# Value product from three fp16 products of high and low parts, with the low part made on VectorE

## What is computed

```python
A  = einsum('mi,bhis->bhms', Wa, xh) + ba
Bm = einsum('ni,bhis->bhns', Wb, xh) + bb
V  = einsum('ni,bhis->bhns', Wv, xh) + bv
attn_maps = softmax(Bm, axis=-1)       # over the pixels
attn_vecs = softmax(V, axis=2)         # over the 64 channels of a head
G = einsum('bhms,bhns->bhmn', A, attn_maps)
Z = einsum('bhmn,bhns->bhms', G, attn_vecs)
x = x + Z                              # then group norm, filters, add
```

## Time and profile before

| | us |
|---|---|
| median of 3 runs | 14357.67 (14353.88 to 14361.22) |
| profiled execution | 14358.22 |
| its span, first to last instruction | 14356.5 |
| TensorE busy | 13503.8 (94%) |
| ScalarE busy | 11121.4 (77%) |
| GpSimd busy | 9729.7 (68%) |
| VectorE busy | 9540.1 (66%) |

### The profile page before, as it was taken

How to read it: one execution, slowest core, us unless ns; L and a number is a source line. 1 busy time by engine, 2 the same in 40 slices (tenths; PEclk the granted TensorE clock), 3 DMA queues, 4 the chain that set the end, 5 groups by cost and what they waited for, 6 DMA issues and landing times.

```text
span 14356.5 us, 399601 instructions
## 1 busy us (share of the span) xinstructions
PE 13503.8 (94%) x158336; PEld 11965.0 (83%) x158688; DVE 9540.1 (66%) x23485; ACT 11121.4 (77%) x20736; POOL 9729.7 (68%) x16823
## 2 busy tenths in 40 slices
PE   7999999999999999999999999999999999999999
PEld 6888888888888888888888888888888888888888
DVE  6666666666666666666666666666666666666665
ACT  6777777777777777777777877777777777777777
POOL 5666666666666676666766667666676666766667
PEclk9999999999999999999999999999999999999999
DMA  3234222343223432234322343223432234322242
GB/s 90 77 101 108 77 74 76 99 108 81 75 75 95 108 84 75 75 92 108 90 73 75 87 108 93 74 75 86 105 97 75 74 83 105 102 73 75 78 105 58
DMA packets 1998658, 1242.80 MB, mean 87 GB/s; under 512 B 79748, under 2 KB 1931140, under 8 KB 1996804
## 3 DMA queue, kind: packets, MB, share of 16 engines
q1 hardware_dynamic: 1996804, 1217.21, 32.6%
HBM read 570.85 MB, written 268.44 MB: 58 GB/s over the span
## 4 chain that ended last, share of the span: by engine, by line
PE 65%; DVE 18%; ACT 11%; issue 6%; SPq 0%; DMA 0%; POOL 0%; DVEq 0%; POOLq 0%
PE ps L1145 64%; DVE nblk L870 4%; ACT t L664 4%; DVE t L1046 3%; ACT yb L696 3%; DVE z L1052 2%; DVE nrun L874 2%; DVE srun L858 2%; ACT z L679 2%; DVE mrun L859 2%; ACT xn L669 1%; DVE pt L864 1%; DVE bexp L877 1%; ACT yr L702 1%; PE ps L1197 0%
## 5 line engine op out<-in xcount | busy, mean ns | idle before, releaser
L1145 PE MATMUL ps<-dn_t,yb 128*128 128x64 f32 (+1 forms) x32768 | 5057.5, 255 | 0.0
L1145 PEld LDWEIGHTS ps<-dn_t,yb 128*128 128x128 f32 x32768 | 4701.4, 191 | 18.4 <-issue 14.8
L494 POOL TENSOR_SCALAR yb<-yb 128x532 f32<-128x532 f32 x4096 | 2587.1, 632 | 1761.9 <-ACT yb L696 1740.9
L1046 DVE TENSOR_TENSOR t<-ps,t 128x266 f16<-128x266 f32 x4096 | 1752.5, 432 | 2698.9 <-ACT t L664 2595.8
L1145 PE MATMUL ps<-up,xn 128*128 128x266 f16 x12288 | 3275.1, 278 | 50.8 <-DVE t L1046 11.2
L664 ACT ACTIVATE t<-ps 128x266 f16<-128x266 f32 x4096 | 1589.1, 393 | 2099.9 <-PE ps L1145 2044.0
L696 ACT ACTIVATE yb<-ps,bias_b 128x532 f32<-128x532 f32 x4096 | 2860.4, 699 | 56.9 <-PE ps L1145 51.9
L1145 PE MATMUL ps<-up_a,t 128*128 128x138 f16 x15360 | 2030.1, 223 | 310.4 <-DVE t L1046 309.5
L1052 DVE TENSOR_TENSOR z<-ps,z 128x512 f16<-128x512 f32 x2048 | 1416.5, 692 | 943.1 <-ACT z L679 898.3
L1145 PE MATMUL ps<-up_b,p 128*128 128x138 f16 x15360 | 2023.3, 223 | 0.0
L1145 PEld LDWEIGHTS ps<-up,xn 128*128 128x128 f16 x12288 | 1724.8, 141 | 228.6 <-DVE t L1046 125.5
(11 more groups left out here) (168 smaller groups left out, 27876.5 us busy)
## 6 DMA issues: line engine op xcount, KB each, us to landing
xc<-in_x SPq DMA_DIRECT2D x512, 512.0 KB, 4.7
xh<-in_x SPq DMA_DIRECT2D x480, 512.0 KB, 5.7
p<-t SPq DMA_DIRECT2D x1920, 128.0 KB, 2.5
out<-xh SPq DMA_DIRECT2D x480, 512.0 KB, 3.2
t<-t SPq DMA_DIRECT2D x960, 128.0 KB, 2.5
xn<-in_x SPq DMA_DIRECT2D x64, 512.0 KB, 5.1
xh<-in_x SPq DMA_DIRECT2D x64, 256.0 KB, 3.0
out<-xh SPq DMA_DIRECT2D x64, 256.0 KB, 2.6
```

Of the source, the lines that this page charges most:

```text
L494: nc.gpsimd.tensor_scalar(v, v, CLAMP, -CLAMP, ALU.min, ALU.max).then_inc(s_yc, 1)
L1046: nc.vector.tensor_tensor(t1[:, par, 1, i, :], ps[:, bank, 0:UP], t1[:, par, 0, i, :], ALU.subtract).then_inc(s_t1, 1)
L1145: return nc.tensor.matmul(o, l, r, start=start, stop=stop, skip_group_check=share)
```

## The change

The block is now normalised fully when it is gathered: `centre` has `scale=r0, bias=nmr0`, so the weights need no scaling, and `wvs`, `wvh` and their two instructions a unit go. The weights are split once, at the program's start, into `wv_2`: high part in fp16, low part the fp16 of the rest. `cast` writes the block's high part in fp16 into `xcs[r][:, 0]`. A new step of VectorE, `value_low`, writes the low part, `xcb[r]` minus the high part, into `xcs[r][:, 1]`, and a new semaphore `s_xw` tells of it. `value` waits for that and makes high x high, low weights x high, high weights x low, each in fp16 with 512 columns. `v_t` takes the high parts. The buffers lie in a half of `t1` that the stage doesn't use.

```diff
...
             def attention(u):
...
                 def centre(k, r):
                     act.activation(xcb[r].rearrange("p (w h) -> p w h", w=WB), xc_wh[:, bass.ts(k, WB), :], ACT.Identity,
-                                   bias=nm0).then_inc(s_xv, 1)
+                                   scale=r0, bias=nmr0).then_inc(s_xv, 1)
 
                 def cast(k, r):
                     act.wait_ge(s_xv, NBLK * u + k + 1)
-                    act.activation(xb_[r % 2][:].rearrange("p w h -> p (w h)"), xcb[r], ACT.Copy).then_inc(s_xb, 1)
+                    act.activation(xcs[r][:, 0, :], xcb[r], ACT.Copy).then_inc(s_xb, 1)
...
+            nc.vector.tensor_copy(wv_2[:, 0, :], wv2[:])
...
+            nc.vector.tensor_tensor(wv_2[:, 1, :], wv2[:], wv_2[:, 0, :], ALU.subtract)
...
-                nc.vector.tensor_scalar(wbs[:], wb2[:], r0, None, ALU.mult)
-                link(nc.vector.tensor_scalar(wvs[:], wv2[:], r0, None, ALU.mult), done + 5)
+                link(nc.vector.tensor_scalar(wbs[:], wb2[:], r0, None, ALU.mult), done + 5)
 
             def norm0_bias(n, done):
-                nc.vector.tensor_copy(wvh[:], wvs[:])
...
+            def value_low(u, k, r):
+                dve.wait_ge(s_xb, NBLK * u + k + 1)
+                nc.vector.tensor_tensor(xcs[r][:, 1, :], xcb[r], xcs[r][:, 0, :], ALU.subtract).then_inc(s_xw, 1)
+
...
                 if before(1):
                     value_max(u, k, par)
+                if after(1):
+                    value_low(u, k + 1, (r + 1) % RING)
                 if before(2):
                     norm_z(u, k - 2, par)
...
                     if k == NBLK - 1:
+                        value_low(u, 0, 0)
                         value_max(u, 0, 0)
                     add_block(NBLK * u + k, k)
...
                     for w in range(WB):
-                        last = mm(vt_ps[par][:, w * P:(w + 1) * P], xb_[par][:, w, :], wvh[:], False, True,
-                                  share=True)
+                        last = mm(vt_ps[par][:, w * P:(w + 1) * P], xcs[r][:, 0, w * P:(w + 1) * P], wv_2[:, 0, :],
+                                  False, True, share=True)
                     last.then_inc(s_vt, 1)
 
                 def value(k, r):
-                    pe.wait_ge(s_xv, NBLK * u + k + 1)
-                    mm(v_ps[r % 2], wvs[:], xcb[r], True)
+                    pe.wait_ge(s_xw, NBLK * u + k + 1)
+                    mm(v_ps[r % 2], wv_2[:, 0, :], xcs[r][:, 0, :], True, True, share=True)
+                    mm(v_ps[r % 2], wv_2[:, 1, :], xcs[r][:, 0, :], False, True, share=True)
+                    mm(v_ps[r % 2], wv_2[:, 0, :], xcs[r][:, 1, :], False, True, share=True)
...
```

More of the change, by code:

```diff
@@ L100, in attention_then_filters @@
         wbs = sb("wbs", [P, P])
-        wvs = sb("wvs", [P, P])
-        wvh = sb("wvh", [P, P], bf16)
+        wv_2 = sb("wv_2", [P, 2, P], fp16)
         bvs = sb("bvs", [P, 1])
@@ L154, in attention_then_filters @@
         xcb = [xcb_all[:, i * BS:(i + 1) * BS] for i in range(RING)]
+        xcs_all = t1[:, 1, :, :, :].rearrange("p t i u -> p (t i u)")
+        xcs = [xcs_all[:, i * 2 * BS:(i + 1) * 2 * BS].rearrange("p (t s) -> p t s", t=2) for i in range(RING)]
         xlate = xn_2[:, :, :, :, :].rearrange("p a t i w -> p (a t i w)").bitcast(fp32).rearrange("p (c w) -> p c w", w=W)
@@ L216, in attention_then_filters @@
         s_xv = sem("xc_block_centred")
-        s_xb = sem("xc_bf16_ready")
+        s_xb = sem("xc_block_high")
+        s_xw = sem("xc_block_low")
         s_vt = sem("v_transposed_in_psum")
@@ L1204, in attention, with v_t @@
             def attention(u):
-                def v_t(k, par):
+                def v_t(k, par, r):
                     pe.wait_ge(s_xb, NBLK * u + k + 1)
@@ L1228, in attention @@
                     sum_block(NBLK * u + NBLK - 2 + k, k)
-                    v_t(k, k)
+                    v_t(k, k, k)
                 value(0, 0)
@@ L1254, in values @@
                     if after(2):
-                        v_t(k + 2, par)
+                        v_t(k + 2, par, (r + 2) % RING)
                 steps(pe, NBLK, RING, values)
```

## The result

| | median us (runs) | against before, 95% interval |
|---|---|---|
| before | 14355.77 (4) | |
| changed | 14940.74 (14939.35 to 14941.95, 4) | 1.0409 (1.039 to 1.0427) |

The changed kernel is 4.1% slower; 14950 us were forecast. The profiled execution has a span of 14937.6 us. By the profile's page, VectorE went from 9540.1 to 10745.8 us busy and TensorE from 13503.8 to 13421.9.

A forecast was written before the change was run, and what follows sets the result against it. TensorE was taken to bound the value stage at 2.51 us a block, then value_low's wait for GpSimd's add at 3.12. (17.1 for periods + 1.5 for the head) x 32 = 595 us on 14358.2 gives 14950, range 14560 to 15180.

The forecast's parts named there:

- The bound: Value stage before the change: TensorE sets the pace at 2.51 us a block, with three other engines close behind.
- The sums of 2.26 and 2.36: Value stage after the change: TensorE's path falls to 2.26 us a block, ScalarE's step rises to 2.36.
- The wait: VectorE's value_low, with two SBUF inputs, waits every block for GpSimd's running add and ends about 0.54 us after it.
- The period: Value stage, 28 blocks a unit: add, value_low and normalisation in turn give 3.12 us a block, 0.61 more than before.
- The head: Start of the value stage, up to the first normalisation: 1.5 us more a unit, over 32 units.
- The 0.61 for value_low(0): Head of the stage: value_low of block 0, ahead of the last sums, adds 0.61 us before the addition into gaug.
- Products and columns: Three fp16 value products take 0.66 us where one fp32 took 0.91; centre's added scale column costs about 97 ns.
- A: Rival: a 512-element value_low does not wait for GpSimd's add; VectorE bounds at 2.38 us a block, 14290 us; chance 0.08.
- B: Rival: at the add's end GpSimd's spread goes ahead of value_low; period 3.66 us, 15440 us; chance 0.07.
- C: Rival: GpSimd falls one block behind; add, value_low and spread in turn, period 2.7 us, 14580 us; chance 0.04.
- D: Rival: the fp16 products are slower than the bf16 row of the same width; chance under 0.01.
- The sign that the chain would lie on VectorE and GpSimd: Expected in the changed kernel's trace: the value stage's chain of waits lies on VectorE and GpSimd.

The follow-up runs named there:

- three_nolow: The changed kernel without value_low; TensorE still makes three fp16 products, the third repeating the low weights by the high part; 14267.3 us, 0.9947 of before.
- late: The changed kernel with value_low moved behind the normalisation of block k-2 in VectorE's queue; 14512.6 us, 1.0113 of before.
- one_elem: The kernel before plus a one-element VectorE tensor_tensor, both inputs in SBUF, behind each value-stage maximum, result unused; 14449.9 us, 1.0070 of before.
- memset: one_elem with GpSimd's add replaced by a write-only memset of 1800 fp32 elements, lasting 1.60 us; 14347.7 us, 0.9995 of before.
- cast_one: The changed kernel with value_low a one-input copy from SBUF to SBUF, fp32 to fp16; third product repeats the low weights; 14694.6 us, 1.0236 of before.
- psum_in: swap with value_low's first input read from PSUM from block 2 on, third product repeating the low weights; 14441.5 us, 1.0064 of before.
- small_add: The changed kernel with GpSimd's add over 128 of each block's 512 elements; 14371.4 us, 1.0019 of before.
- swap: The changed kernel with value_low of block k+1 put ahead of the maximum of block k on VectorE; 15487.6 us, 1.0793 of before.

## Why the prediction held

- *The bound.* TensorE held the stage, and with less work there the next bound was near: three_nolow's mean period is 2.43, only 0.08 below (from the reciprocals of blocks 0 and 28 at 599.35 and 667.38), on ScalarE and TensorE in turn. The sums of 2.26 and 2.36 were both a little short of that.
- *The wait.* The prediction read it off one-element instructions of other steps, and it came as described: value_low ends 0.53 after the add, 0.54 forecast. Its size was off. The forecast has 0.8 us of waiting and some 1.3 in all; the held value_low waits 663.16 - 662.18 = 0.98 and lasts 1.51. Two terms were mixed up there: the 0.8 is when VectorE comes to value_low, counted from the end of the normalisation, and not how long it then waits; from the add's start it comes after 0.69 by the earlier trace rows, which leaves 0.96. The sum of the period only uses the add's end, so the time didn't suffer. Nor does each of the 28 wait: in the second unit the low parts of blocks 30 and 31 take 0.68 and 0.69 (the latter at 709.92), because an aggregation of 0.79 us (L938) stands ahead of them and the add is over. With it, VectorE's own work makes 3.13 and 3.14 there as well, which the forecast hadn't foreseen: those two periods are right by luck.
- *The period.* 3.12 forecast, 3.13 measured. 28 x 0.62 x 32 = 556 us of the 585.
- *The head.* From the addition into gaug to the first reciprocal 3.24 was forecast (0.21 + 3.03) and 3.21 measured (before: 2.32). The 0.61 for value_low(0) ahead of it was too much. From the update of mrun to the addition into gaug it is 619.76 - 615.56 = 4.20 us; before it was 604.26 less the 600.24 of this row:

```profile
600.24 0.34 DVE L859 SCALAR_TENSOR_TENSOR mrun<-mrun,alpha,ps 128x128 f32<-128x128 f32 x1
```

  That is 4.02, so value_low(0) costs 0.18 and not 0.61 (the other units are alike); VectorE had been waiting there, and the wait ahead of `xbart`, for one, fell from 0.64 to 0.42. So of the 18.3 us a unit, 17.3 are the periods, 0.9 the head behind gaug and 0.2 what lies ahead of it; the stretch from block 28 to block 31 gives back another 0.2 (6.55 us against 6.73).
- *Products and columns.* 0.65 for the value product (0.66), 1272 ns for centre (1270).
- *Rivals.* A (no wait for 512 elements) is refuted by value_low's 1.51 us. B (the spread first) by the spread's 1.08: it was ready at the add's end, yet it ended behind value_low, which had asked 0.9 us before it. C (GpSimd a block behind) did not come about here; late is the order that comes near it, with 2.60 where C had 2.7. D was refuted by 0.65. The granted clock stayed at 1.00 with TensorE busy 78% of the stage. The sign that the chain would lie on VectorE and GpSimd did not show as such: the chain has no line of GpSimd, whose add lies hidden in value_low's duration.
- *The rule* of the Trainium skill that was weighed ("SBUF — State Buffer", section "Who interferes with whom") agrees with every run: two inputs in SBUF wait (one_elem), a write-only instruction of GpSimd doesn't hold them (memset), a copy within SBUF waits as well (cast_one), one input from PSUM doesn't (psum_in), and it holds both ways (late). In the earlier trace rows, in the changed kernel, in late and in the pairs of small_add, the one that asked first went first.

## What to carry to other kernels

Before work is moved to VectorE, sort its operands. In the rows read here a tensor_tensor with two inputs in SBUF, and a copy from SBUF to SBUF, were held each time they met GpSimd's add or spread, which read SBUF. Add their times to GpSimd's, not only to VectorE's: add, value_low and spread in turn were summed to 2.66 us by rival C, late shows 2.60, and the order of the queues decides how far above that the period lies. A one-element instruction of a known kernel whose duration jumps beside GpSimd's shows the price beforehand. Where such a step must be, its place in the queue is worth as much as its length: 3.72, 3.13 and 2.60 us a block for the same instruction in three places, least where it comes just before GpSimd's next long instruction.

## What was not expected of the hardware

- The wait takes in the fixed part of the held instruction: value_low alone is 0.68 to 0.69 long, but ends 0.53 to 0.56 after what held it (changed kernel, swap, late); the one-element one ends 0.02 after. The prediction counted on this from the one-element rows; that it holds for 512 elements was new.
- An fp32 to fp16 copy of 512 elements takes 414 ns at its shortest, and still costs more beside the add (1.25 us) than a tensor_tensor with a PSUM input (0.69 us).
- A difference of 0.01 us in the start decides which engine is held and whether one period is 2.29 or 2.92 us (small_add), and yet the mean over many stays at 2.43, as other engines set it.
